# Paired one-hot codes in the sorting stage, a late reload of x for the residual, and a counting stage in which ScalarE makes 27 of 45 source codes

## What is computed

```python
h = jnp.maximum(_layernorm(x, axis=-1), 0.0)         # x is 1024 x 512
x = x + _ref(h, edge_index, cond, ...)

def _gcn(x, src, dst, W, b, n):                      # src, dst: edges and self loops
    deg = segment_sum(ones, dst); dinv = deg ** -0.5
    norm = dinv[src] * dinv[dst]
    return segment_sum((x @ W)[src] * norm[:, None], dst) + b

def _ref(x, ...):
    x_in = x
    h = batch_norm(x); h = _gcn(h, ..., gcn_in_w)
    for i in range(4):
        h = h + attention(layernorm(h), cond)
        h = h + geglu_mlp(layernorm(h))
    h = _gcn(h, ..., gcn_out_w)
    return h + x_in                                  # so the result is h + relu(LN(x)) + x
```

## Time and profile before

| | us |
|---|---|
| median of 3 runs | 2566.85 |
| lowest and highest | 2565.05, 2567.74 |
| the profiled execution, whole | 2565.13 |
| its span in the profile | 2563.3 |
| PE busy of the span | 2485.3 (97%) |
| DVE, ACT, POOL busy | 1378.1, 1040.9, 596.4 |

### The profile page before, as it was taken

One profiled execution on the slowest core, in us unless ns is written; L12 is line 12 of the kernel. 1 busy time (PEld: TensorE's weight loads), 2 busy tenths in 40 slices (PEclk: granted clock), 3 DMA queues, 4 the chain that ended last, 5 costly groups with the idle time before them and its releaser, 6 DMA issues.

```text
span 2563.3 us, 35706 instructions
## 1 busy us (share of the span) xinstructions
PE 2485.3 (97%) x12583; PEld 2057.7 (80%) x12583; DVE 1378.1 (54%) x2824; ACT 1040.9 (41%) x2058; POOL 596.4 (23%) x466
## 2 busy tenths in 40 slices
PE   5959999999999999999999999999999999999999
PEld 2517888888888888888888888888888888888887
DVE  8997676642225667642225776622236677622245
ACT  8874434362223443552223344542224434632222
POOL 3000000034441000144430000154440000154431
PEclk7879999999999999999999999999999999999999
DMA  2002000011121000011110000012110000021130
GB/s 107 1 31 106 17 33 17 33 58 63 61 70 50 17 33 33 25 69 64 65 61 34 34 27 23 34 66 66 65 64 24 33 33 33 26 82 65 60 118 34
DMA packets 30806, 124.13 MB, mean 48 GB/s; under 512 B 3152, under 2 KB 3536, under 8 KB 26064
## 3 DMA queue, kind: packets, MB, share of 16 engines
q1 hardware_dynamic: 30672, 122.41, 13.7%
HBM read 116.10 MB, written 6.29 MB: 48 GB/s over the span
## 4 chain that ended last, share of the span: by engine, by line
PE 90%; DVE 6%; ACT 3%; issue 1%; DMA 0%; DVEq 0%; POOL 0%; SPq 0%; ACTq 0%
PE ps L1468 28%; PE ps L1469 27%; PE ps L1470 27%; PE ps L1652 2%; PE ps L1669 2%; PE ps L1671 2%; DVE oh_d L1111 1%; PE ps L1666 1%; DVE oh_s L1109 1%; ACT full L767 1%; PE ps L1679 1%; PE ps L1693 1%; ACT oh_d L630 1%; DVE xT_lo L1366 0%; ACT xT_hi L773 0%
## 5 line engine op out<-in xcount | busy, mean ns | idle before, releaser
L1468 PE MATMUL ps<-xT_hi,wg_hi 128*128 128x512 f32 (+1 forms) x1104 | 414.3, 375 | 1.9 <-DVE xT_lo L1366 1.9
L1469 PE MATMUL ps<-xT_lo,wg_hi 128*128 128x512 f32 (+1 forms) x1104 | 412.6, 374 | 0.0
L1470 PE MATMUL ps<-xT_hi,wg_lo 128*128 128x512 f32 (+1 forms) x1104 | 412.5, 374 | 0.0
L1410 DVE SCALAR_TENSOR_TENSOR ff<-ps,cols_sb,gel 128x512 f32<-128x512 f32 x128 | 96.0, 750 | 574.0 <-ACT gel L863 574.0
L863 ACT ACTIVATE gel<-ps,cols_sb 128x512 f32<-128x512 f32 x128 | 88.1, 688 | 629.9 <-PE ps L1470 629.9
L1419 DVE TENSOR_TENSOR h<-h,ps 128x512 f32<-128x512 f32 x256 | 174.9, 686 | 136.7 <-PE ps L1470 136.7
L1468 PEld LDWEIGHTS ps<-xT_hi,wg_hi 128*128 128x128 f32 x1104 | 207.8, 188 | 39.5 <-DVE xT_lo L1366 2.7
L1469 PEld LDWEIGHTS ps<-xT_lo,wg_hi 128*128 128x128 f32 x1104 | 207.8, 188 | 36.8
L1470 PEld LDWEIGHTS ps<-xT_hi,wg_lo 128*128 128x128 f32 x1104 | 207.7, 188 | 36.6
L420 POOL TENSOR_SCALAR veps<-mv 128x1 f32<-128x1 f32 x65 | 14.1, 218 | 939.0 <-DVE mv L929 939.0
L1468 PE MATMUL ps<-cond_hi,w_hi 128*128 128x512 f32 x512 | 203.7, 398 | 0.0
(11 more groups left out here) (250 smaller groups left out, 5389.1 us busy)
## 6 DMA issues: line engine op xcount, KB each, us to landing
stage<-in_pieces SPq DMA_DIRECT2D x138, 512.0 KB, 3.3
stage<-in_condT SPq DMA_DIRECT2D x33, 1024.0 KB, 4.8
x<-in_x SPq DMA_DIRECT2D x2, 1024.0 KB, 7.3
res_s<-x SPq DMA_DIRECT2D x2, 1024.0 KB, 4.3
at_s<-at SPq DMA_DIRECT2D x1, 2048.0 KB, 10.9
at16b<-at_s SPq DMA_DIRECT2D x1, 2048.0 KB, 9.8
out<-h SPq DMA_DIRECT2D x8, 256.0 KB, 2.0
bias_row<-in_rows SPq DMA_DIRECT2D x6, 256.0 KB, 3.4
```

The source lines that it names most:

```text
L1410: dve.scalar_tensor_tensor(ff[:, s % 2, :], ps[:, step_bank(j, a, s, 0), :], cols_sb[:, bass.ds(COL["geglu_b"] + 32 * l + 4 * j + 2 * a + ...
L1468: pe.matmul(bank, l_hi, r_hi, start=(first and i == 0), stop=False)
L1469: pe.matmul(bank, l_hi, r_lo, start=False, stop=False)
L1470: end = pe.matmul(bank, l_lo, r_hi, start=False, stop=(last and i == n - 1))
```

## The change

It does the following:

- `scatter`: one scalar_tensor_tensor of 128 by 256 writes both codes of a chunk side by side into `oh_d`, with `lane` as its pointer scalar and the two weights as a broadcast second tensor. Before, two tensor_scalar of 128 by 128.
- `d_square` and `d_equal` on ScalarE (2 instructions of 4096 columns, 8 of 1024) become 2 comparisons of 4096 columns on VectorE, behind chunks 3 and 5.
- `x_sum`, the store to `res_s`, its two waits on ScalarE and one on VectorE go. `y_of` moves from ScalarE to VectorE. The hand-written chunk numbers move: the second four transposes from 16 to 14, degree matmuls from 36 to 26, `y_low` from 50, 57, 64, 71 to 47, 51, 55, 59, the 8 `g_product` from 76 every 6 chunks to 66 every 7.
- Tail: x is loaded a second time from its input (2 DMAs, as large and at the same place as the loads of `res_s` before); ScalarE normalizes 8 tiles (L594's form), VectorE makes relu and sum in 8 instructions (L1000's form), behind the preparation of the last aggregation.
- Counting: ScalarE makes the codes of j % 5 in (1, 3, 4) in every flush, 27 of 45 (before: the odd j of the first flush, 22, and the odd j from round 16 on of the others, 14 or 15). The square of the next code is issued before the weighing of this one.
- `fix` goes: readers take the low 16 bits of the rounded float as the digit.

```diff
         def coded_by_scalar(j):
-            return j % 2 == 1 and (j < FLUSH or j % FLUSH >= 2 * RING)
+            return j % 5 in (1, 3, 4)
+        def digit(words):
+            return words.bitcast(i16).rearrange("p (n two) -> p n two", two=2)[:, :, 0]
@@ sync
-            for half in range(2):
-                r = slice(half * NT // 2, (half + 1) * NT // 2)
-                sp.wait_ge(x1_ok, (half + 1) * NT // 2)
-                sp.dma_start(res_s.rearrange("(t p) d -> p t d", p=P)[:, r, :], x1[:, r, :])\
-                  .then_inc(res_out[half], 16)
...
-                sp.dma_start(bits(buf[:, 3]), res_s.rearrange("(t p) d -> p t d", p=P)[:, r, :])\
+                sp.dma_start(buf[:, :, :], x.rearrange("(t p) d -> p t d", p=P)[:, r, :])\
                   .then_inc(res_in[half], 16)
@@ scalar, sorting stage
-                if 16 <= c < 20:
-                    d_square(d_high[:, 32 * (c - 16):32 * (c - 15), :], c - 14, 2)
-                if c in (20, 21, 26, 27):
-                    n = (20, 21, 26, 27).index(c)
-                    d_equal(d_high[:, 32 * n:32 * n + 32, :], n + 2)
-                if 22 <= c < 26:
-                    x0T_of(c - 18)
+                if 18 <= c < 22:
+                    x0T_of(c - 14)
...
-                if c in (46, 53, 60, 67):
-                    y_of((c - 46) // 7)
-                if c in (47, 54, 61, 68):
-                    y_high((c - 47) // 7)
-                if c in range(86, 123, 6):
+                if c in (45, 49, 53, 57):
+                    y_high((c - 45) // 4)
+                if c in range(74, CHUNKS, 7):
@@ scalar, counting stage
-                def fix(t):
-                    act.wait_ge(a_round, NT * f + t + 1)
-                    act.activation(place[t], place[t], ACT.Copy, bias=-ROUND).then_inc(a_digit, 1)
...
+                code_square(coded[0])
+                for j, ahead in zip(coded, coded[1:]):
+                    code_square(ahead)
+                    code_weigh(j)
@@ scalar, tail
+            for t in range(NT):
+                act.wait_ge(res_in[t // (NT // 2)], 16)
+                act.activation(z_end(t), x_end(t), ACT.Identity, scale=x_rstd[:, t:t + 1], bias=x_nm[:, t:t + 1])\
+                    .then_inc(x_end_ok, 1)
@@ vector, sorting stage
-                for a, place in enumerate((oh_s[:, c % RING, :], oh_d[:, c % RING, 2 * P:3 * P])):
-                    last = dve.tensor_scalar(place, iota0[:, 0:P], lane[:, c:c + 1], pay[:, a, c:c + 1],
-                                             ALU.is_equal, ALU.mult)
-                last.then_inc(oh_ok, 1)
+                dve.scalar_tensor_tensor(oh_d[:, c % RING, 2 * P:4 * P].rearrange("p (a n) -> p a n", a=2),
+                                         iota0[:, 0:P].unsqueeze(1).broadcast_to([P, 2, P]), lane[:, c:c + 1],
+                                         pay[:, :, c:c + 1].broadcast_to([P, 2, P]), ALU.is_equal, ALU.mult)\
+                    .then_inc(oh_ok, 1)
...
-                if c in range(14, 14 + 2 * NT, 2):
-                    x_sum((c - 14) // 2)
...
+                if c in (3, 5):
+                    d_equal((d_low, d_high)[(c - 3) // 2][:, :, :], (c - 3) // 2 + 1)
...
+                if c == 43:
+                    y_of(0)
+                if c in (47, 51, 55, 59):
+                    y_low((c - 47) // 4)
+                    if c < 59:
+                        y_of((c - 43) // 4)
+                if c in range(80, 123, 7):
+                    xs_low((c - 80) // 7)
@@ vector, tail, behind the last xs_lo
+                    for t in range(NT):
+                        dve.wait_ge(x_end_ok, t + 1)
+                        dve.scalar_tensor_tensor(z_end(t), z_end(t), 0.0, x_end(t), ALU.max, ALU.add).then_inc(x1_ok, 1)
@@ tensor
-                if c in range(76, 76 + 6 * NT, 6):
-                    t = (c - 76) // 6
+                if c in range(66, 66 + 7 * NT, 7):
+                    t = (c - 66) // 7
```

More of the change, by code:

```diff
@@ L601, in x0T_of @@
                     .then_inc(x0T_ok, 1)
[L603 to L609, removed]
             def y_high(k):
@@ L691, in a_digits, with code_square, code_weigh @@
                         high(t)
[L693 to L697, removed]
+            def code_square(j):
                 if j >= 2 * RING:
                     act.wait_ge(oh_used, CHUNKS + j - 2 * RING + 1)
-                act.activation(place, iota0[:, 0:P], ACT.Square, bias=minus_of[:, j:j + 1]).then_inc(code_ok, 1)
-                act.wait_ge(code_ok, 2 * codes_by_scalar(j) - 1)
+                act.activation(ring_of(j)[0][:, j % RING, :], iota0[:, 0:P], ACT.Square, bias=minus_of[:, j:j + 1])\
+                    .then_inc(square_ok, 1)
+            def code_weigh(j):
+                place = ring_of(j)[0][:, j % RING, :]
+                act.wait_ge(square_ok, codes_by_scalar(j))
                 act.activation(place, place, ACT.Relu, scale=minus_w[:, j:j + 1], bias=srt[:, 2, j:j + 1])\
@@ L706, in _ @@
             for f in range(FLUSHES):
-                for j in range(FLUSH * f, FLUSH * (f + 1)):
-                    if coded_by_scalar(j):
-                        code(j)
-                    if j == FLUSH + 30:
+                coded = [j for j in range(FLUSH * f, FLUSH * (f + 1)) if coded_by_scalar(j)]
+                code_square(coded[0])
+                for j, ahead in zip(coded, coded[1:]):
+                    code_square(ahead)
+                    code_weigh(j)
+                    if f == 1 and j == coded[len(coded) // 2]:
                         for n in range(2, 4):
                             w_high(n, n % 2, attn_place(0, 0, n % 2))
+                code_weigh(coded[-1])
                 a_digits(f)
@@ L995, in _ @@
                 .then_inc(strip_ok, 1)
-            def x_sum(t):
-                dve.wait_ge(x0_ok, t + 1)
-                dve.scalar_tensor_tensor(x1[:, t, :], z1[:, t, :], 0.0, x1[:, t, :], ALU.max, ALU.add)\
-                    .then_inc(x1_ok, 1)
             def batch_stats():
@@ L1050, in first_w_low, with d_equal, y_of @@
                                   ALU.subtract).then_inc(w_ok, 1)
+            def d_equal(place, n):
+                dve.wait_ge(d_apart_ok, n)
+                dve.tensor_scalar(place, place, 0.0, None, ALU.is_equal).then_inc(d_oh_ok, 1)
+            def y_of(k):
+                if k == 0:
+                    dve.wait_ge(bn_ok, 3)
+                else:
+                    dve.wait_ge(y_lo, k)
+                dve.tensor_scalar(full[:, :, :].rearrange("p a n -> p (a n)"), x0T[:, k, :], bn[:, k:k + 1],
+                                  bn[:, KC + k:KC + k + 1], ALU.mult, ALU.add).then_inc(bnf_ok, 1)
             def y_low(k):
@@ L1146, in _ @@
                 one_hots(j)
-                if j in (1, 4):
-                    xs_low(6 + (j - 1) // 3)
+                if j == 1:
+                    xs_low(NT - 1)
                 if j in (80, 83):
@@ L1151, in _ @@
                 if j >= FLUSH and j % FLUSH == 2 * RING - 1:
-                    if j // FLUSH == 1:
-                        for half in range(2):
-                            dve.wait_ge(res_out[half], 16)
                     for t in range(NT):
@@ L1514, in _ @@
                 pe.wait_ge(oh_ok, c + 1)
-                for a, code in enumerate((oh_s[:, c % RING, :], oh_d[:, c % RING, 2 * P:3 * P])):
+                for a, code in enumerate((oh_d[:, c % RING, 2 * P:3 * P], oh_d[:, c % RING, 3 * P:4 * P])):
                     last = pe.matmul(ps[:, a, 0:SLOTS + 1], code, oh_d[:, c % RING, 0:SLOTS + 1],
```

92 lines of the change are left out of this document (38 added, 54 removed).

## The result

| us | before | after |
|---|---|---|
| median | 2566.38 (5 runs, 2565.05 to 2567.74) | 2551.62 (5 runs, 2551.40 to 2552.04) |
| the profiled execution, whole | 2565.13 | 2551.45 |
| its span | 2563.3 | 2549.6 |

The changed kernel takes 0.9944 of the time (95% interval 0.9933 to 0.9954). It is 14.8 us faster by the medians and 13.7 by the two profiled executions; 12.7 was forecast.

The account below looks back on a forecast made before the run. VectorE was taken to bound up to the first product, TensorE the products, VectorE the counting. The early stages' 12.7 us off the profiled 2565.13 gave 2552.4; 1.7 up to the median gave 2554.1, forecast 2554, range 2547 to 2562.

Parts of the forecast that it names:

- The order of the limits: Before 188.6 us: VectorE to the first product, TensorE through the products, then VectorE; the 2237 us behind stay.
- The paired code: In `scatter`, one scalar_tensor_tensor costs 0.41 us a chunk against 0.445 for two instructions, 4.5 us over 128 chunks.
- The rival of half rate: In `scatter`, the paired code costs 0.68 us; 27.5 us lost, 2582 us; chance 0.07.
- Rival 4: In `scatter`, the paired code's pointer is free, 0.33 us each; 2.5 us more gained, 2551.6 us; chance 0.07.
- Up to the first product: In sorting, statistics begin at 38.7 us and the first product at 70.2 instead of 77.51, 7.3 us earlier.
- Products: At the end of sorting, TensorE bounds with 3.63 us a period; end at 102.5 instead of 107.11, 4.6 earlier.
- Flushes: In counting, cuts at 125.0, 151.0 and 176.9 us instead of 128.51, 156.47 and 188.60; sum 12.7 us gained.
- Rival 1: In counting, separating square and weighing gains nothing, a pair stays at 0.82 us; 5.0 us gained, 2562 us; chance 0.12.
- Rival 2: In counting, TensorE at 1.2 GHz becomes the bound; 13.6 us lost against 12.7 gained, 2568 us; chance 0.06.
- the largest item: In the second flush, VectorE takes digits at 151.7 us against 162.59, 10.9 earlier, with 54 source codes instead of 84.
- Tail: At the kernel's end, the added ScalarE and VectorE instructions cost 0 us; 13 us of VectorE's idle gap are left.

Follow-up runs that it names:

- the 24 additions: The changed kernel with 24 unused additions of 128 by 512 on VectorE ahead of its residual sums in the tail: median 2553.01 us, ratio 0.9949.
- the four rounds: The changed kernel with `y_of` on ScalarE and source codes of rounds 112, 117, 122 and 127 moved from VectorE to ScalarE: median 2550.92 us, ratio 0.9939.

## Why the prediction was right

**The order of the limits.** VectorE, TensorE, VectorE in turn, and the layers untouched: as put down.

**The paired code.** 0.41 was taken, and four codes stand in 1.58 us of the chain after, 0.40 each. The rival of half rate (2582) is out: 478 ns for 256 columns are the 419 of one column a nanosecond and 59 for the pointer, where up to 76 had been allowed. The rule in the Trainium skill (Vector Engine (DVE) Microarchitecture Reference, Points that are easy to get wrong) would have made it 0.68 by the prediction's working; that differs from the measurement, for a float16 and a float32 source as well, and the measurement decides. Rival 4, a free pointer, is out too.

**Up to the first product.** Statistics at 38.16 (38.7 forecast) and the first product at 69.55 (70.2). `y_of` took 812 ns and cost 0.73 in a row (54.68 to 55.41), the two-columns-a-cycle end of its bounds. The two comparisons on VectorE took 1.22 each, where 1.2 was taken between bounds of 0.7 and 4.3 that no row narrowed; that choice was a guess, and it held. (Its terms for VectorE's arrival add up to 36.1, not 36.3, which changes nothing.)

**Products.** Period 3.68 (3.63), the end of sorting 102.05 (102.5).

**Flushes.** Cuts at 123.88, 148.69 and 176.07 (125.0, 151.0, 176.9), takes at 126.57, 150.83 and 176.70 (127.1, 151.7, about 177.6). The pair on ScalarE came out at 0.68 where 0.70 was taken; over 27 codes that is 0.5 a flush, and the earlier end of sorting is another 0.5. Rival 1 is out by the run without interleaving: 0.82 there, 0.68 here; its price of 7.7 was close to the 7.3 that this run lost. Rival 2 is out: the granted clock was 0.79 as before. (Its price was some 2 us too high in the first flush: the rows show 512-column matmuls 0.43 apart at the low level, not 0.46.)

In the second flush two errors fell on different engines. From its first cut to its second, ScalarE needed 24.8 us (148.69 - 123.88) where 26.0 was summed; from the end of its first takes to its second, VectorE needed 19.4 (131.4 to 150.83) where 18.2 was summed. The two were forecast level, so the later of them came out 0.9 early; that it came so near is in part luck.

**What the prediction did not see.** It named a price for each of the three edits of the counting stage: 1.0 us for `fix`, 7.7 for a failed interleaving, and the split as the reason of the largest item. The runs show that there is no such price. Removing `fix` alone gives 1.3 us of the counting stage, any pair 1.2 to 2.1, and all three 8.5, while putting `fix` back into the changed kernel costs 7.3 of the stage and 8.0 of the span (the split alone and the interleaving alone were not tried). VectorE was late by 6 to 7 us in the first two flushes; the split takes that off it, but ScalarE then needs 27 codes at 0.82, or 1.0 us a bank for cut and fix, and is late itself. Only with both removed does it keep up. The sum was right because it was made for the whole, engine by engine, to the later of the two: it starts ScalarE's second flush at 129.0, 4.0 behind the first cut, and so holds what the missing `fix` gives there, though it never says that this is most of its worth.

**Tail.** 0 as forecast, by the trace: from the first take of the third flush to the end of the span it is 2372.9 us, against 2373.1. The cover is larger than the 13 us named, as the trace with the 24 additions shows.

**Ahead of the forecast.** The surplus is 1.0 us by the spans (13.7 against 12.7), 0.45 of it at the end of sorting and 0.4 in the counting stage. By the medians it is 2.1, because the profiled execution before, which the forecast started from, lies 1.3 below the median of its kernel (below).

## What to carry to other kernels

Where two engines share a stage, an edit that relieves one is worth no more than what the other engine has left in hand: compute both engines' ends for each combination, and expect edits to be worth little alone and much together. Put a dependent instruction one place later, with an independent one between, before you look for a cheaper form of either. Cover for work ahead of a paced stream is the gap plus what the engine can catch up in the stream.

## What the runs showed of the hardware that I had not expected

**The clock rises at a point that moves.** In the kernel after, TensorE is granted its full clock, 2.4 GHz, from 20 to nearly 38 us, 0.50 of it, which is 1.2 GHz, from 38 us up to the first product, and the full clock again within or right behind that product. Matmuls of the same form around that point, first in the kernel after, then in the one with `w_low` on GpSimd:

```profile
71.58 0.59 PE L1457 MATMUL ps<-w_hi,w_lo 128*128 128x512 f32 x1
72.00 0.40 PE L1455 MATMUL ps<-w_hi 128*128 128x512 f32 x1
```

```profile
76.21 0.55 PE L1457 MATMUL ps<-w_hi,w_lo 128*128 128x512 f32 x1
77.42 0.47 PE L1455 MATMUL ps<-w_hi 128*128 128x512 f32 x1
```

By the granted clock the rise comes at 72.0 in the first, 2.7 us behind the start of the product (69.30), and at 76.5 in the second, 5.2 behind (71.37). The first product took 4.1 us in the one and 5.2 in the other. Five kernels with the same sorting stage (after, not interleaved, old split, fix back, additions in the tail) had the rise 2.7, 4.1, 3.2, 3.3 and 2.5 us behind the start of the product, which itself stood between 69.26 and 69.72, and ended sorting between 102.05 and 102.69. The two numbers account for the third: matmuls stand 0.43 apart at the low level and 0.23 at the high one, so each microsecond of product at the low clock costs 0.46, and the start with 0.46 of the delay gives the differences of these five ends within 0.03 us (an estimate from their rows). Two others alike in the stage (`y_of` on ScalarE, without and with the four rounds) ended it at 100.85 and 101.41, with the rise at 71.3 and 72.6. So half a microsecond to one of a step ahead of the first product can't be read from the end of sorting in one trace, unless 0.46 of the delay of the rise is taken off first. The profiled execution of before has its rise at 79.4, only 2.1 us behind the start of its product (77.32), and lies 1.3 below the median of its kernel; in the two runs of that kernel without `fix`, and with the new split, the rise came at 81.8 and 81.7, 4.5 behind, and sorting ended 1.0 later. What sets the point stays open.

**GpSimd can stop VectorE altogether**, for 2.1 us at a time here. Beside GpSimd's small step on 128 by 4 numbers (1.13 us, at 43.89 in the trace of after) the codes ran on at 0.4 us each. Whether the width or the operation makes the difference was not tried.
